# The low halves of the attention probabilities, shared between VectorE and GpSimd

## The reference

```
q, k, v = (qkv[0], qkv[1], qkv[2])
attn = jax.nn.softmax(jnp.einsum('bhsd,bhtd->bhst', q, k) * SCALE, axis=-1)
out = jnp.einsum('bhst,bhtd->bhsd', attn, v)
```

## Time and profile before

| quantity | value |
|---|---|
| time, median of 3 runs | 2971.27 us (2967.63 to 2975.25) |
| the profiled execution's own time | 2969.1 us |
| its span, first to last instruction | 2967.3 us |
| mean granted TensorE clock in it | 0.955 |
| busy in the span: PE, DVE, POOL, ACT | 89%, 53%, 43%, 26% |
| line 736, low halves on POOL | 360 instructions, 322.4 us, 928 ns each |
| line 2057, A on PE | 1080 instructions, reading PF (720) or PL (360) |
| probability stage of the first pair | 2257.0 to 2318.4 us of the span |

### The profile page before, as it was taken

How to read it: one execution, slowest core, us unless ns; L and a number is a source line. 1 busy time by engine, 2 the same in 40 slices (tenths; PEclk the granted TensorE clock), 3 DMA queues, 4 the chain that set the end, 5 groups by cost and what they waited for, 6 DMA issues and landing times.

```text
span 2967.3 us, 65252 instructions
## 1 busy us (share of the span) xinstructions
PE 2651.6 (89%) x22950; PEld 1938.8 (65%) x22950; DVE 1584.1 (53%) x2845; ACT 777.7 (26%) x1100; POOL 1277.2 (43%) x1363
## 2 busy tenths in 40 slices
PE   5998999978998769999999898876769999999999
PEld 4787888847676557888885667754545556555555
DVE  7566666664545553333334354544775745746731
ACT  2111121201222212111220132211134355354350
POOL 1684211147777710000006677774415274274372
PEclk9999999999999979999999899987979999999999
DMA  5233333459989932333237988997310000000013
GB/s 165 90 127 103 121 123 118 146 197 314 321 298 307 313 126 90 104 121 99 94 99 251 331 291 302 323 339 241 96 38 1 22 22 1 22 22 1 22 48 94
DMA packets 102525, 440.92 MB, mean 149 GB/s; under 512 B 19881, under 2 KB 20204, under 8 KB 98081
## 3 DMA queue, kind: packets, MB, share of 16 engines
q0 software_dynamic: 55712, 266.88, 26.4%
q1 hardware_dynamic: 44001, 131.65, 13.8%
q10 hardware_dynamic: 2592, 39.32, 3.7%
HBM read 357.66 MB, written 80.08 MB: 148 GB/s over the span
## 4 chain that ended last, share of the span: by engine, by line
PE 59%; DVE 16%; issue 7%; POOL 7%; DVEq 4%; DMA 4%; ACT 2%; POOLq 0%; SPq 0%; ACTq 0%
PE PS L1709 26%; PE PS L2057 6%; PE PS L1719 3%; PE PS L1987 3%; PE PS L1808 3%; POOL GATA L685 2%; PE PS L1902 2%; DVE NMC L1630 2%; PE PS L2044 2%; PE PS L1846 2%; POOL ROW L685 2%; PE PS L2045 2%; POOL PL L736 2%; PE PS L1840 2%; PE PS L1860 1%
## 5 line engine op out<-in xcount | busy, mean ns | idle before, releaser
L1709 PE MATMUL PS<-WHL,XT 128*125 (+1 forms) x2880 | 487.2, 329 | 7.1 <-DVE WHL L1092 4.2
L1709 PE MATMUL PS<-WHL,HT 128*125 (+1 forms) x2880 | 477.1, 329 | 12.0 <-DVE HT L1245 9.4
L1709 PEld LDWEIGHTS PS<-WHL,HT 128*125 (+1 forms) x2880 | 395.3, 138 | 90.1 <-DVE HT L1245 10.6
L1709 PEld LDWEIGHTS PS<-WHL,XT 128*125 (+1 forms) x2880 | 390.8, 137 | 82.9 <-issue 4.7
L736 POOL TENSOR_TENSOR PL<-PF 125x500 bf16<-125x500 f32 (+1 forms) x360 | 322.4, 928 | 216.4 <-ACT PF L949 215.5
L685 POOL DMA_INDIRECT GATA<-msg_table,SKEY x324 | 311.1, 960 | 138.2 <-issue 96.1
L1179 DVE SCALAR_TENSOR_TENSOR MSG<-PS,MSG 125x768 f16<-125x768 f32 x160 | 153.0, 956 | 360.8 <-ACT MSG L775 358.9
L775 ACT ACTIVATE MSG<-PS 125x768 f16<-125x768 f32 x160 | 129.6, 810 | 794.7 <-PE PS L1709 794.7
L2057 PE MATMUL PS<-PF,V 125*128 125x500 bf16 (+1 forms) x720 | 244.6, 352 | 16.0 <-POOL PL L736 14.4
L685 POOL DMA_INDIRECT ROW<-msg_table,SKEY x216 | 213.0, 986 | 83.6 <-issue 59.6
L949 ACT ACTIVATE PF<-PS,QK 125x500 f32<-125x500 f32 (+1 forms) x360 | 213.5, 608 | 124.3 <-PE PS L2045 118.1
(11 more groups left out here) (316 smaller groups left out, 4803.4 us busy)
## 6 DMA issues: line engine op xcount, KB each, us to landing
msg_table<-MSG SPq DMA_DIRECT2D x160, 336.0 KB
WST<-in_wg_dram ACTq DMA_DIRECT2D x16, 2304.0 KB, 9.9
WST<-in_wf_dram SPq DMA_DIRECT2D x7, 1536.0 KB, 6.8
KROW<-key_rows POOLq DMA_DIRECT2D x54, 192.0 KB, 3.8
WST<-in_wm_dram SPq DMA_DIRECT2D x6, 1152.0 KB, 5.5
msg_table<-MSG SPq DMA_DIRECT2D x160, 39.0 KB
GATA<-msg_table,SKEY POOLq DMA_INDIRECT x324
ROW<-msg_table,SKEY POOLq DMA_INDIRECT x216
```

The lines of the kernel that those rows point to most:

```text
L1709: ins = pe.matmul(PS[0:ROWS, b0 + h, 0:HALF], X[:, xp, k, bass.ts(t, ROWS)], panel_part(slot, wp, k, h), start=k == 0 and xp + wp == 0, st ...
```

## The change

Of the 60 tiles of a pair, the 20 with n % 3 = 2 get their low half from VectorE; GpSimd makes the other 40. VectorE signals with a new semaphore, `ffn_lo2`, and TensorE waits ahead of A n for the one or the other. VectorE's instruction is the same subtraction of the same shape. Where it stands in VectorE's queue is set by the new lines in the loop over `LOWS`: ahead of the normalisation that follows A 9 of a chunk stand the tiles up to four beyond that chunk's last tile. So ahead of O00 stand tiles 2, 5, 8, 11; ahead of O01 tiles 14, 17, 20, 23; ahead of O02 tiles 26, 29, 32; ahead of O10 tiles 35, 38, 41; ahead of O11 tiles 44, 47, 50, 53; ahead of O12 tiles 56, 59.

```diff
@@ GpSimd
                     if n_ == SPLIT_AT - 4:
                         ffn_scales()
+                    if n_ % 3 == 2:
+                        continue
                     g.wait_ge(S["ffn_act"], ffn.taken(it, f"S{h}{c}{t}"))
@@ VectorE
+                def low_part(n_):
+                    h, c, t = n_ // 30, n_ // 10 % 3, n_ % 10
+                    n = CHUNKS[c][1]
+                    v.wait_ge(S["ffn_act"], ffn.taken(it, f"S{h}{c}{t}"))
+                    v.tensor_tensor(PL[:, n_ % PARTED, 0:n], PF[:, n_ % PARTED, 0:n], PH[:, n_ % PARTED, 0:n, 1], ALU.subtract).then_inc(S["ffn_lo2"], 1)
...
+                    h = int(r[1])
+                    if r[0] == "O":
+                        for n_ in range(2, 2 * 3 * RT, 3):
+                            k = 10 * (3 * h + int(r[2])) + 9 + LAG
+                            if k - 10 < n_ <= k or (r == "O00" and n_ <= k) or (r == "O12" and n_ > k):
+                                low_part(n_)
                     v.wait_ge(S["ffn_pe"], ffn.made(it, r))
-                    h = int(r[1])
@@ TensorE
-                        pe.wait_ge(S["ffn_lo"], it * 60 + (k + 1))
+                        if k % 3 == 2:
+                            pe.wait_ge(S["ffn_lo2"], it * 20 + (k // 3 + 1))
+                        else:
+                            pe.wait_ge(S["ffn_lo"], it * 40 + (k - k // 3 + (1 if k % 3 < 2 else 0)))
```

More of the change, by code:

```diff
@@ L250, in graph_and_attentions_kernel @@
             rf_in mw_in mw_top mw_scale mw_hi mw_lo hf_out hf_in mix_pe mix_act mix_dve vec_in jr_in0 jr_in1 jr_in2 jr_in3 jr_in4 jr_in5 hf_made jr_made mp_done mp_free js_done js_sd ln_made
-            lg_in lg_pe lg_free gate_in gate_ex gate_done qk_scale s_scale rank_top rank_row rank_one rank_all rank_scale lt_pe lt_free lt_low ffn_ready ffn_pe ffn_dve ffn_act ffn_hi ffn_lo tops_made av_done row_in
+            lg_in lg_pe lg_free gate_in gate_ex gate_done qk_scale s_scale rank_top rank_row rank_one rank_all rank_scale lt_pe lt_free lt_low ffn_ready ffn_pe ffn_dve ffn_act ffn_hi ffn_lo ffn_lo2 tops_made av_done row_in
             or_in0 or_in1 or_free or_made ob_in fp_done fp_free out_free out_out x2_out0 x2_out1 x2_made xf_made xf_t xf_hi xf_free""".split()
```

## The result

| | kernel before | changed kernel |
|---|---|---|
| median | 2969.45 us (2967.39 to 2975.25, 4 runs) | 3015.44 us (3012.73 to 3019.79, 4 runs) |
| ratio | 1 | 1.0153, 95% interval 1.0133 to 1.0173 |
| the profiled execution: span | 2967.3 us | 3018.0 us |
| first O00 to the end of the span | 696.8 us | 737.0 us |

The change made the kernel slower by 46 us. The forecast was 3006 us, 2990 to 3026. The last line of the table takes out the scatter of what comes before the changed code: it is the span less the start of the first O00, 2967.3 - 2270.5 and 3018.0 - 2281.0. In it the change costs 40.2 us. The other 10.5 us of difference between the two spans lie ahead of the first pair's first exponential (2257.9 and 2268.4 us), where both programs do the same; from there to the first O00 both take 12.6 us.

The account below looks back on a forecast made before the run. TensorE was taken to set the pace, losing 14.4 us to low tiles. Waits of 0.5 + 1.3 + 5.1 + 1.0 - 2.05 - 0.2 a pair gave 33.9 us, the clock 4, on 2969.1: 3007, written 3006 us (2990 to 3026).

Parts of the forecast that it names:

- A 14 behind O00: TensorE waits for low 14, queued on VectorE behind normalisation O00: late by 0.2 to 1.1 us, taken 0.5.
- A 26 behind low 23 and O01: TensorE waits for low 26, queued on VectorE behind low 23 and O01: late by 1.3 us, 0.9 to 1.9.
- A 44 behind O10 and the split: TensorE waits for low 44, queued behind O10 and the weight split: 4.0 us unhindered, up to 6.7, taken 5.1.
- O11 to O12, the lateness at A 56: Low 56 queued behind O11 stretches O11 to O12 from 5.28 to 6.3 us: late by 1.0.
- A 48, wait for GpSimd: With 20 tiles fewer, GpSimd's backlog goes, and TensorE's 2.05 us wait a pair ahead of A 48 with it.
- A 38: Where ScalarE is late, low 38 itself gets shorter on VectorE: gain 0 to 0.3 us, taken 0.2.
- clock, six pairs: Longer idling at A 44 drops TensorE's clock in all six pairs instead of two: +4 us, bounds -5.6 and +15.
- Rival A: VectorE's and GpSimd's tiles do not hinder each other: 22 us of waits in all, 2991 to 2995 us; chance 0.13.
- the split's last instruction: Sign expected in VectorE's weight split: its last instruction takes 2.6 instead of 3.28 us.
- rival B: The clock loses more: twice the slow stretch at A 44 and one more fall a pair, 3027 us; chance 0.10.
- Rival D: Relief of GpSimd at A 48 and A 38 and of the clock outweighs: 19 us faster, 2950 us; chance 0.02.
- C: Hand-over between VectorE and GpSimd binds the narrow tiles: 22 us more, 3028 us; chance 0.04.

Follow-up runs that it names:

- tile 44 back: Changed kernel with tile 44 returned from VectorE to GpSimd; 3000.95 us, ratio 1.0086 to the kernel before.
- fifteen early tiles: Changed kernel with tiles 14, 26, 44, 47 and 56 returned to GpSimd, VectorE keeping 15; 2968.54 us, ratio 0.9963 to the kernel before.
- five tiles with the split first: Changed kernel with only tiles 38, 39, 40, 42, 43 on VectorE and the weight split ahead of O10; 2960.78 us, ratio 0.9945 to the kernel before.

## Why the prediction was right, point by point

The working is the forecast's; beside its terms, in us a pair, stands what the changed kernel's rows showed.

| term | forecast | measured |
|---|---|---|
| A 14 behind O00 | 0.5 | 0.42 |
| A 26 behind low 23 and O01 | 1.3 | 1.15 |
| A 44 behind O10 and the split | 5.1 | 5.05 |
| O11 to O12, the lateness at A 56 | 6.3 instead of 5.28 | 6.30 (2328.48 to 2334.78) |
| A 48, wait for GpSimd | gone (-2.05) | gone |
| A 38 | -0.2 | -0.3 |
| all of these, six pairs | +33.9 | +35.7 (TensorE's idle time) |
| clock, six pairs | +4, falls in all of them | +4.5 (TensorE's busy time), falls in all of them |
| sum over the stages | +38 | +40.2 |

**The waits.** All four came at the places named, and elsewhere TensorE's order kept its pace: from A 26 to A 37 it takes 10.92 us before and now. The step that carries the result is the third, a tile behind O10 and the split; the split moved behind low 47 shows it by itself, since nothing else was changed there.

**A 44 was right in size for a composition that was partly wrong.** The forecast has two pieces of waiting for GpSimd here: 0.37 us in line 991 (now 993), which was to pay 0.97, and 0.9 for low 48, which was to go between the split and low 44. The rows show them elsewhere. Line 993 took 0.62, unhindered. Low 48 got in at line 995, which took 3.48 instead of 2.62 us, and low 44 then followed at once with 0.67. And low 41 was held for 0.86 us (1.54 instead of 0.68), by which O10 began some 0.4 us late (with tile 44 back, where no wait falls between, A 44 comes 4.45 us after the start of O10, against 4.86 before); that was not foreseen. So 1.27 us were counted and about 1.26 came (0.86 and 0.4), the amount by which the wait shrank when GpSimd read nothing. That the two sums agree so closely is luck. The part of the queue is not: 4.0 us by the forecast without any hindrance, 3.79 measured.

**The ports.** Rival A, no mutual hindrance, falls: VectorE's tiles took up to 1.545 us, and without GpSimd's reads 0.681 at the most. The forecast had 13 us between itself and A; the experiment gave 8.3 in the stretches from O00 to O12. The Trainium skill ("SBUF — State Buffer", section "Who interferes with whom") says that a VectorE instruction with two SBUF inputs contends with a GpSimd instruction that reads SBUF and not with one that only writes it; both halves of that sentence agree with these two figures, 1.545 and 0.681 us. One sign did not come: the split's last instruction was to take 2.6 us instead of 3.28, and took 3.48, because a GpSimd tile still came beside it.

**The clock.** The fall came in every pair, as rival B had it too, but not a second one in each; in four of the pairs the stretch at the lower level was longer, most of the added part in TensorE's idle time ahead of A 44, where it costs little: these four pairs take 53.91 to 53.96 us from O00 to O12, the other two 53.76 and 53.81. The stretch from O10 to O12 came to 23.37 to 23.57 us, within the 23 to 25 forecast. What the clock costs can be read from TensorE's busy time from O00 to O12: 43.5 us in the pairs of the kernel before that had no fall, 44.8 to 44.9 in its other four, 45.0 to 45.3 now. So a fall cost 1.5 to 1.7 us a pair now and 1.3 to 1.4 before, where the forecast had 1.6 and 1.4.

**The difference between 37 and 46 us.** The stages gave 40.2 instead of 38, and the rest of the timed difference lies ahead of them in these executions or in the scatter of the runs; the interval of the ratio, 1.0133 to 1.0173, is 39.5 to 51.4 us and so holds the 40.2.

**Rival D** asked what the relief alone is worth, and priced it at 19 us. The fifteen early tiles gave 9.7 of it, and the five tiles with the split first 16.2. So the relief is real, at least in part. In the change the place of the 20 tiles in VectorE's queue cost more than it gave.

**C** did not come: GpSimd idled between tiles, and TensorE waited 49.1 us for VectorE's tiles and 2.2 for GpSimd's.

## What to carry to other kernels

A piece of work that is handed to an engine with time to spare arrives late when something long stands ahead of it in that engine's queue: compare its place with the moment at which the reader wants it, item by item, not the engine's busy share (VectorE was busy for 53% of the span here, and TensorE waited 49.1 us for it). Where some items fall behind a long piece, give the engine those that don't, or move the long piece to where nothing urgent stands behind it. Here five well-placed tiles with the split moved gained 16.2 us and fifteen tiles 9.7, while twenty lost 40.2. And before sharing work between VectorE and GpSimd where both read SBUF, count up to one instruction of the other engine as waiting: here a VectorE tile of 0.68 us took up to 1.545 beside GpSimd tiles of 1.02.

## What the runs showed of the hardware that I had not expected

A GpSimd fill, which writes SBUF and reads nothing, lengthened none of the VectorE subtractions: 36 of the 120 ran beside a fill, and the longest took 0.681 us. Beside GpSimd subtractions they took up to 1.545. And the start of the first O00 lay anywhere from 2270.5 to 2283.4 us in nine profiles, though the programs are the same up to the first pair's first exponential, some 12 us ahead of it. That is more than most of the differences sought; in a single execution only the time from there on could tell the kernels apart, and differences under 5 us not even by that.
